# Query norms in four column tiles, a second output tile, and the query projection behind the gate products

## The reference

```python
Q = (query @ Wq.T + bq)            # 16 heads of 16 channels
C_Q = max(|Q|^2 + |L|^2 - 2 Q.L, 0) # L: the 64 landmarks (keys at landmark_idx)
Phi_Q = exp(-C_Q / temperature)
Y = solve(W_kernel, Phi_K^T V)      # once per batch and head
out = (Phi_Q @ Y) / max(Phi_Q @ solve(W_kernel, sum Phi_K), 1e-10)
x = layernorm(x + out @ Wo.T + bo)
logits = x @ Wg.T + bg              # top 2, softmax over the two
x = layernorm(x + sum_selected w_e * (x @ We[e].T + be[e]))
```

## Time and profile before

| | |
|---|---|
| median of three runs | 2059.63 us |
| the profiled execution | 2053.05 us |
| its span | 2051.3 us |
| TensorE busy over the span | 1835.4 us, 89% |
| VectorE busy | 1577.8 us, 77% |
| ScalarE busy | 1230.0 us, 60% |
| GpSimd busy | 930.2 us, 45% |
| mean granted clock of TensorE | 0.967 |

### The profile page before, as it was taken

The page is one execution under the profiler, slowest core; times in us unless marked ns, Lnnn a source line. Parts: engine busy times, 40 slices in busy tenths (PEclk is TensorE's granted clock), DMA queues, the critical chain, the costliest instruction groups (busy, mean ns, idle before and its releaser), DMA issues.

```text
span 2051.3 us, 41908 instructions
## 1 busy us (share of the span) xinstructions
PE 1835.4 (89%) x15928; PEld 1351.7 (66%) x15928; DVE 1577.8 (77%) x3316; ACT 1230.0 (60%) x2411; POOL 930.2 (45%) x1179
## 2 busy tenths in 40 slices
PE   4488999999967999999999999999999999999997
PEld 3177878778753666666666666666666666666665
DVE  5678844997336788888888888888888888888874
ACT  2265666676654475667557666656755756675553
POOL 2300000000002466666666666666666666656666
PEclk9689999999986999999999999999999999999999
DMA  2676687777862333333342334333334333233300
GB/s 82 106 171 147 160 191 166 169 166 184 171 184 65 88 85 85 86 80 83 93 102 74 88 78 100 75 98 85 81 77 103 87 84 92 73 89 87 88 26 21
DMA packets 184637, 213.95 MB, mean 104 GB/s; under 512 B 57692, under 2 KB 108276, under 8 KB 184180
## 3 DMA queue, kind: packets, MB, share of 16 engines
q1 hardware_dynamic: 184244, 210.75, 42.8%
q0 software_dynamic: 192, 0.52, 0.1%
HBM read 61.26 MB, written 23.59 MB: 41 GB/s over the span
## 4 chain that ended last, share of the span: by engine, by line
PE 48%; DVE 25%; DMA 10%; issue 8%; SPq 5%; ACT 2%; POOL 1%; DVEq 0%; POOLq 0%; ACTq 0%
PE bank L298 11%; PE bank L300 10%; PE bank L299 10%; DMA out<-y_out 8%; PE bank L1623 6%; PE bank L1483 2%; PE bank L1593 2%; PE bank L1499 2%; PE bank L1484 2%; DVE inversion L1048 2%; DVE if L1249 2%; DVE phi L1020 2%; DVE y_out L1291 1%; DVE y_out L1290 1%; DVE inversion L1050 1%
## 5 line engine op out<-in xcount | busy, mean ns | idle before, releaser
L298 PE MATMUL bank<-weh,x1h 128*128 128x512 f32 x1024 | 430.7, 421 | 34.3 <-DVE y_out L1291 33.7
L300 PE MATMUL bank<-wel,x1h 128*128 128x512 f32 x1024 | 405.3, 396 | 0.0
L299 PE MATMUL bank<-weh,x1l 128*128 128x512 f32 x1024 | 405.3, 396 | 0.0
L837 ACT ACTIVATE part_x<-bank,gate 128x256 f32<-128x256 f32 x512 | 211.4, 478 | 211.3 <-PE bank L300 207.2
L545 POOL TENSOR_TENSOR x_tok<-x_tok,bo_sb 128x1024 f32<-128x1024 f32 x32 | 76.8, 2400 | 522.9 <-DMA x_tok<-in_x 522.9
L298 PEld LDWEIGHTS bank<-weh,x1h 128*128 128x128 f32 x1024 | 192.7, 188 | 147.7 <-DVE y_out L1291 55.0
L782 ACT ACTIVATE phi<-bank,nlt_cur,invt 128x512 f32<-128x512 f32 x256 | 187.3, 795 | 77.0 <-PE bank L1593 77.0
L637 ACT ACTIVATE phi<-bank,invt 128x512 f32<-128x512 f32 x256 | 162.5, 685 | 102.2 <-PE bank L1484 102.0
L300 PEld LDWEIGHTS bank<-wel,x1h 128*128 128x128 f32 x1024 | 192.9, 188 | 46.3
L299 PEld LDWEIGHTS bank<-weh,x1l 128*128 128x128 f32 x1024 | 193.5, 189 | 33.8
L557 POOL TENSOR_TENSOR part_x<-part_x 128x512 f32<-128x512 f32 x128 | 183.5, 1434 | 8.5 <-ACT part L837 8.5
(11 more groups left out here) (191 smaller groups left out, 4577.7 us busy)
## 6 DMA issues: line engine op xcount, KB each, us to landing
x_raw<-in_xT SPq DMA_DIRECT2D x64, 512.0 KB, 5.6
q_stack<-kh SPq DMA_DIRECT2D x256, 128.0 KB, 2.4
x_tok<-in_x SPq DMA_DIRECT2D x32, 512.0 KB, 4.1
q_stack<-kl SPq DMA_DIRECT2D x128, 128.0 KB, 2.4
q_stack<-augk SPq DMA_DIRECT2D x32, 512.0 KB, 4.5
out<-y_out SPq DMA_DIRECT2D x64, 256.0 KB, 2.6
k_hl<-attn_h SPq DMA_DIRECT2D x32, 256.0 KB
k_ha<-attn_h SPq DMA_DIRECT2D x32, 256.0 KB
```

What stands on the lines that cost most here:

```text
L298: nc.tensor.matmul(outp, ah, bh, start=first, stop=False)
L299: nc.tensor.matmul(outp, al, bh, start=False, stop=False)
L300: return nc.tensor.matmul(outp, ah, bl, start=False, stop=last)
L837: last = nc.scalar.activation(parts[t % 2][q - 1][:, u * D:(u + 1) * D], bank[2 + q % 2][:, u * D:(u + 1) * D], ACT.Copy, scale=gate[at][: ...
```

## The change

Three edits, all in the query stage:

1. `query_norms` on TensorE uses eight products of 128 columns in four column tiles, as the key stage does (`quarter_norms`). VectorE then works on 128 x 128 (`key_hi`, `key_aug`) in place of 32 x 512, and SyncE copies the norms into `q_stack` in four pieces of 128 tokens in place of one.
2. A second output tile `y_spare`: chunks with odd p use it. `combine` waits for the store of chunk p - 2, which has a semaphore for each tile and half.
3. The order. On TensorE the gate products come directly behind experts 10, `queries(q+1)` behind them, and `attention(q, 1)` behind experts 11. On VectorE `finish(p, 1)` and `gates_begin(c)` come ahead of `queries_lo(q+1)` and `norm_begin(q, 1)`. On ScalarE `weigh(p, 10)` and `attn_hi(q, 0)` come ahead of `queries(q+1)`, and `gate_exp(c)` directly behind it, ahead of the landmark copies and `weigh(p, 11)`.

```diff
             def query_norms(c):
                 if past_end(c):
                     return
                 dve.wait_ge(qnorm_done, c + 1)
-                norm_rows(augk[0][0:32, :], bank[6]).then_inc(qaug_done, 1)
+                own.then(V.tensor_copy(key_hi[:], bank[6][:, 0:P]))
+                V.scalar_tensor_tensor(key_aug[:], raw(key_hi[:]), lo_sign, bank[6][:, 0:P], ALU.mult,
+                                       ALU.add).then_inc(qaug_done, 1)
...
-                dve.wait_ge(res_stored, 32 * p + 16 * (t // 2) + 16)
-                a = y_out[:, t]
+                if p >= 2:
+                    dve.wait_ge(res_stored[p % 2][t // 2], 16 * (p // 2))
+                a = y_out[p % 2][:, t]
...
+            def quarter_norms(dst):
+
+                for s in range(KC):
+                    for t in range(TPC):
+                        last = mm(dst[32 * t:32 * t + 32, 0:P], neg_block[:, s, :], sq[:, s, t * P:(t + 1) * P],
+                                  start=(s == 0), stop=(s == KC - 1))
+                return last
...
                 pe.wait_ge(ql_done, 2 * (c + 1))
-                square_norms(bank[6]).then_inc(qnorm_done, 1)
+                quarter_norms(bank[6]).then_inc(qnorm_done, 1)
...
                 sp.wait_ge(qaug_done, c + 1)
-                sp.dma_start(raw(q_stack[96:128]), rep(raw(augk[0][0:32, :]), 1, PAIRS)).then_inc(q_stacked, 16)
+                for t in range(TPC):
+                    sp.dma_start(raw(q_stack[96:128, :, t * P:(t + 1) * P]),
+                                 rep(raw(key_aug[32 * t:32 * t + 32, :]), 1, PAIRS)).then_inc(q_stacked, 16)
...
                     weigh(p, 9, me)
-                    queries(q + 1)
                     weigh(p, 10, me)
                     attn_hi(q, 0)
+                    queries(q + 1)
+                    gate_exp(c)
                     if q_ends_batch(cc, b):
                         landmarks_of_batch(b + 1, 0)
                         landmarks_of_batch(b + 1, 1)
                     weigh(p, 11, me)
-                    gate_exp(c)
...
                     x1_lo(c, nxt)
+                    finish(p, 1)
+                    gates_begin(c)
                     queries_lo(q + 1)
                     norm_begin(q, 1)
-                    finish(p, 1)
-                    gates_begin(c)
                     combine(p, 3, me)
...
                     experts(p, 9, me)
+                    experts(p, 10, me)
+                    gate_logits(c, nxt)
                     queries(q + 1, 1)
-                    experts(p, 10, me)
+                    experts(p, 11, me)
                     attention(q, 1)
-                    gate_logits(c, nxt)
-                    experts(p, 11, me)
                     experts(p, 12, me)
```

More of the change, by code:

```diff
@@ L120, in program @@
         sq = sb("sq", [P, KC, CH])
-        augk = [sb("augk0", [64, CH], f32r)]
-        aug_hi = sb("aug_hi", [32, CH], f32r)
+        with nc.sbuf_tensor("augk0", [64, CH], f32r) as augk0, nc.sbuf_tensor("aug_hi", [32, CH], f32r) as aug_hi:
+            augk = [augk0]
+        y_spare = sb("y_spare", [P, TPC, D])
+        key_hi, key_aug = sb("key_hi", [P, P], f32r), sb("key_aug", [P, P], f32r)
         phi = sb("phi", [P, 8, CH])
@@ L153, in program @@
             l_hh, l_lo = [[sb1(f"l_{n}0", [P, GROUPS, 4, NL], f32r)] for n in ("hh", "lo")]
-            key_hi, key_aug = sb1("key_hi", [P, P], f32r), sb1("key_aug", [P, P], f32r)
             with ExitStack() as setup:
@@ L167, in program @@
                 a.append(sb1(f"l_{n}1", [P, GROUPS, 4, NL], f32r))
-        x_tok, y_out = sb("x_tok", [P, TPC, D]), sb("y_out", [P, TPC, D])
+        x_tok, y_out = sb("x_tok", [P, TPC, D]), [sb("y_out", [P, TPC, D]), y_spare]
         x1 = [sb(f"x1_{i}", [P, TPC, D]) for i in range(2)]
@@ L182, in program @@
         winv_sb, y_cur = sb("winv_sb", [64, H, NL]), sb("y_cur", [P, PAIRS, 64])
-        we_raw = [a[:].rearrange("p t d -> p (t d)") for a in (*x1, y_out, part)]
+        we_raw = [a[:].rearrange("p t d -> p (t d)") for a in (*x1, y_out[0], part)]
         idx_loaded, small_loaded, w_loaded, we_loaded = (sem("idx_loaded"), sem("small_loaded"), sem("w_loaded"),
@@ L228, in program @@
             sem("ffn_done"), sem("comb_done"), sem("part_ready"), sem("part_sum"), sem("acc_done"), sem("ln2_stats"), sem("ln2_coef"),
-            sem("res_ready"), sem("res_stored"))
+            sem("res_ready"), [[sem(f"res_stored{i}{half}") for half in range(2)] for i in range(2)])
         block = ctx.enter_context(nc.Block())
@@ L290, in groups_of @@
             return a[:].rearrange("p (s j) n -> p j s n", s=KC)[:, j]
-        STACKED = 16 * 13
+        STACKED = 16 * 16
         KH_STACKED, AUG_STACKED = 16 * 6, 16 * TPC
@@ L313, in _ @@
             sp.sem_inc(zt_saved, 1)
-            sp.sem_inc(res_stored, 32)
             sp.sem_inc(xqh_ready, 2)
@@ L479, in turn @@
                         sp.dma_start(out_v[bass.ds(p, 1), :, 2 * half:2 * half + 2].rearrange("a p t d -> (a p) t d"),
-                                     y_out[:, 2 * half:2 * half + 2]).then_inc(res_stored, 16)
+                                     y_out[p % 2][:, 2 * half:2 * half + 2]).then_inc(res_stored[p % 2][half], 16)
             for b in range(BATCH - 1):
@@ L484, in _ @@
             turn(BATCH - 1)
-            sp.wait_ge(res_stored, 32 * (NCH + 1))
+            for i in range(2):
+                for half in range(2):
+                    sp.wait_ge(res_stored[i][half], 16 * NCH // 2)
         @block.gpsimd
@@ L843, in result @@
                 act.wait_ge(ln2_coef, TPC * p + t + 1)
-                nc.scalar.activation(y_out[:, t], y_out[:, t], ACT.Identity, bias=nm2[:, t:t + 1],
+                y = y_out[p % 2]
+                nc.scalar.activation(y[:, t], y[:, t], ACT.Identity, bias=nm2[:, t:t + 1],
                                      scale=rs2[:, t:t + 1]).then_inc(res_ready, 1)
@@ L1296, in finish @@
                 dve.wait_ge(comb_done, TPC * p + t + 2)
-                V.tensor_tensor(y_out[:, t], y_out[:, t], parts[t % 2][0][:, 0:D], ALU.add).then_inc(acc_done, 1)
+                y = y_out[p % 2]
+                V.tensor_tensor(y[:, t], y[:, t], parts[t % 2][0][:, 0:D], ALU.add).then_inc(acc_done, 1)
                 dve.wait_ge(acc_done, TPC * p + t + 3)
-                own.then(V.bn_stats(st2[:, t], y_out[:, t]))
+                own.then(V.bn_stats(st2[:, t], y[:, t]))
                 dve.sem_inc(dve_waited, 1)
@@ L1462, in key_norms @@
                     pe.wait_ge(prod_read, done[-1])
-                for s in range(KC):
-                    for t in range(TPC):
-                        last = mm(bank[4][32 * t:32 * t + 32, 0:P], neg_block[:, s, :], sq[:, s, t * P:(t + 1) * P],
-                                  start=(s == 0), stop=(s == KC - 1))
-                last.then_inc(norm_done, 1)
+                quarter_norms(bank[4]).then_inc(norm_done, 1)
             def dists(c, t):
```

## The result

| | before | after |
|---|---|---|
| time, median of the runs | 2058.36 us (4 runs, 2057.1 to 2061.8) | 2119.64 us (4 runs, 2118.7 to 2122.0) |
| span of the profiled execution | 2051.3 us | 2117.2 us |
| mean granted clock of the span | 0.967 | 0.932 |
| granted clock, 1202 to 1971 us | 1.00 | 0.95 |
| mean turn (28 turns, by the copy of the norms) | 43.53 us | 45.67 us |

The changed kernel is slower: ratio 1.0297, 95% interval [1.0279, 1.0315], 61 us.

A forecast was written before the change was run, and what follows sets the result against it. Bound taken: TensorE's own work plus about 2 to 2.7 us of waits per turn. Order, norms, landmark turns and stage ends sum to -7 us, clock falls add 52: +45 on 2059.63, 2104 us, range 2055 to 2132.

The forecast's parts named there:

- The wait ahead of the gate products: TensorE, new order: gate products need `x1_lo` and start at 1230.6, 2.2 us lost in a turn.
- Ahead of experts 10: TensorE, new order: experts 10 comes next and waits for `combine` until 1227.0, 0.6 us lost.
- The clock: TensorE around the gate products: clock falls in nine turns of ten at 2.0 us each, +52 us.
- The first rival: Gate-product wait: the clock holds, 2.2 us being under the harmless 2.30; sum -7 us, 2053 us; chance 0.14.
- The rival of two falls' worth per turn: Gate products: clock falls early in the wait, gates run at half and keep it down; 2140 us; chance 0.10.
- The landmark turns: Landmark copies on ScalarE delay `weigh(p, 11)`; TensorE waits 2.6 us ahead of experts 13 in 7 turns, +18 us.
- Norms: Query-stage norms in four column tiles: TensorE saves 1.28 us a turn, whole if nothing it waits for is late.
- Second tile: `combine`: VectorE's 2.2 us wait for the store goes; TensorE gains 0 to 0.86 us a turn, taken as 0.5.
- Copies of the norms: Four copies into `q_stack` in place of one: no cost taken, 0.6 us a turn left in the range.
- The sum: Whole kernel: -7 us without the clock plus 52 for it, +45 us; 2104 us against 2059.63.

The follow-up runs named there:

- filler ahead: Changed kernel plus eight redundant 512-column products per turn on TensorE, between experts 10 and the gate products; 2061.8 us.
- half the filler: Changed kernel plus four redundant 512-column products per turn ahead of the gate products; 2092.7 us.
- norms and tile: Changed kernel with the old order restored on TensorE, VectorE and ScalarE; four-column-tile norms and second output tile stay; 2027.3 us.
- experts 11 first: Changed kernel with experts 11 moved ahead of the gate products on TensorE; 2092.6 us.
- experts 15 first: "norms and tile" with combine(p, 3) ahead of the index search, experts 15 ahead of gate transposes, experts 0 ahead of bias products, weigh(p, 14) ahead of gates_T; 2024.1 us.

## Why the prediction was right

The forecast was slower, 2104 us in 2055 to 2132; measured were 2119.6. Step by step:

- **The wait ahead of the gate products**: predicted 2.2 us for `x1_lo`, measured 1.91 to 1.93 in all 30 turns. Ahead of experts 10: predicted 0.6 us, measured 0.43 on average, between 0 and 1.1.
- **The clock**: predicted a fall in nine turns of ten at 2.0 us each, +52 us. Measured: a fall behind the wait in 27 of 30 turns, three more at the landmark stall, and 58 us that come back when the wait is filled, 2.0 us a turn. The reason given, that idle time and gate products follow each other directly, is what "filler ahead", "half the filler" and "norms and tile" show together. The first rival (clock holds below 2.30 us) fails on it: 1.9, 1.0 and even 0.5 us were enough here, in 27 of 30, 19 of 29 and 17 of 30 turns. The Trainium skill ("TensorE: Matmul & The Clock Gate", section "Why this matters for your kernels") warns only of idle gaps between bursts of matmuls that are longer than these. By that alone the clock would have held; the 58 us of the filler say otherwise for a gap with narrow products right behind it, and the measurement decides. The rival of two falls' worth per turn is not seen either; only 10 turns had slow gate products as well.
- **The landmark turns**: predicted 2.6 us in 7 turns, +18; measured 2.38 us in the rows, and in the filler kernel, where the clock plays next to no part, these turns are 46.7 us and more against 44.3 in "norms and tile", about 2.4 us, of which a part is that all turns are longer there. What the prediction left out is that the stall can bring a fall too: in four of seven turns, once on top of the one at the gate products.
- **Norms**: predicted -1.28 us a turn, 37 us. The sum on TensorE is right (0.65 us in place of 1.9), but alone the edit gave 14 us: "whole, if nothing it waits for is late" was the step that failed in the old order, since `combine(p, 3)` was late. In the new order the norms and the tile together gave 23 us, so that the 37 us were too much there as well.
- **Second tile**: estimated at 0.5 us a turn, 14 us; measured 17 beside the norms in the old order. The sum has no term of its own for it: it goes from the waits before to those that were forecast. VectorE's wait for the store is gone; that the gain might be lost again in `finish` is not what these runs show.
- **Copies of the norms**: predicted at no cost. They land in 2.5 us by the page, and TensorE waited 5.3 us for them in 17 turns, against 6.0 in 18 before: right. In "experts 11 first" and "experts 15 first" they did bind.
- **The sum**: it is 15 us short of the measured median. The turns say where. Predicted was a mean turn without clock of 43.53 - 0.8 + 0.65 = 43.4 us, and the filler kernel has 43.64; predicted for the clock was 1.8 us per turn, and the difference to 45.67 is 2.03. Both terms are about a quarter of a us too small, 7 us each over the stage. The filler kernel may itself cost a little, so the split is good to some us only. One source is in the working: it takes 2.7 us of waits out of a plain turn of 42.8 us, but the earlier trace rows give 769 - 732 = 37 us in 18 turns, 2.05 us each. With 2.05 the sum is 29 x 0.65 = 19 us higher, 2123 us. That the size came out so near is thus in part luck: what is left out here and the gain of the norms, which was put at least 14 us too high, offset each other.

What stays open: why the falls come in the gate products in one turn and three products later in the next, or not at all, and so what a fall costs in a given turn (1.4 to 3.2 us). Landmark copies in smaller pieces, which might spare the 2.4 us, were not tried.

## What to carry to other kernels

Before moving a wait on TensorE, look at what stands behind it: 1.7 us were free ahead of wide products, and 0.5 to 1.0 us cost a fall of the clock in about six of ten turns ahead of sixteen narrow ones. An order that covers a wait with wide products may look needlessly late and still be the fast one; two short waits can be much cheaper than one of their sum. When a suspected loss is idle time, fill it with redundant products: what comes back although work was added is the clock's part. And split a change into its parts before judging it: this one held 31 us of gain under 92 us of loss.

## What the runs showed of the hardware

- The granted clock fell to its lower level (products of 512 columns 0.43 us apart in place of 0.23) in or behind 16 products of 16 columns, when these had idle time ahead of them: after 1.9 us in 27 of 30 turns, after 1.0 us in 19 of 29, after 0.52 us in 17 of 30. I had expected 1.0 us to be harmless.
- It did not fall after 1.4 to 1.7 us of idle time between products of 512 columns (23 turns), nor in the gate products without idle time ahead (31 turns), nor right behind 1.68 us ahead of the gate transposes (22 turns); behind 1.6 to 1.7 us ahead of the norms' products of 128 columns it fell in 1 of 22.
- Longer idle times did not act the same every time. After 2.6 us ahead of the gate transposes it fell in 16 of 23 turns. After 2.38 to 2.40 us ahead of products of 512 columns it fell in 4 of 7 turns of the changed kernel and in 1 of 7 with the filler, after 3.6 to 3.8 us in 7 of 7 ("experts 11 first").
- Work placed in the idle time raised the speed, and the same work right behind the narrow products did not: 2062 and 2183 us, against 2120 without it.
